# Expert routing of the second layer inside the attention jobs, and expert weights loaded into spent buffers

## The chip, the cores and the metric

The kernel runs on one core of a Trainium2 chip. The metric is the device time of one execution in microseconds (us). Six queues matter: PE (matrix engine; PEld is its weight load), DVE (VectorE), ACT (ScalarE), POOL (GpSimd), and SP, which only issues DMA transfers. ACT and POOL can issue transfers too.

## The reference

Sixteen sequences of 256 tokens with 256 features pass through two layers. Each layer is an attention with a second input, then a gated block of self-attention and experts. Of concern here is the last quarter, the causal self-attention with its mixture of experts:

```
scores = where(causal, q k^T / sqrt(16), min);  o = softmax(scores) v @ w_o     # 16 heads
h      = layernorm(x + o, g1, b1)                       # 4096 rows in all
probs  = softmax(h @ wg);  topv, topi = top_k(probs, 2);  topv /= topv.sum()
y_e    = gelu(h @ w1[e] + bb1[e]) @ w2[e] + bb2[e]      # 8 experts, 256 -> 1024 -> 256, float32
moe    = sum over the 2 chosen experts of topv * y_e
out    = x + tanh(g) * layernorm(h + moe, g2, b2)
```

## The kernel before, in words

**Attention phase** (`attention_phase`). The first three and a half quarters run as 64 jobs: unit u (0 to 3, one for each attention) times sequence b (0 to 15), unit after unit. A job is cut into named steps. `orders()` plans all jobs at once: a greedy list scheduler with a table of costs (`STAGES`) gives every engine a fixed order of steps. Each engine then runs its list strictly in that order and waits on semaphores. Unit 3 is the causal self-attention. Its steps for one sequence: XT, K, Q, V (projections on PE, copied out by ACT), KSPLIT and QSPLIT (POOL cuts a float32 operand into three bfloat16 parts: subtract, cast, subtract), STACKK/STACKQ/ROWSK/ROWSQ (SP writes the parts to memory and reads them back stacked), 16 steps S (scores on PE, masked maximum on DVE), M and MT (maxima folded into the operand), 16 steps T (scores again on PE, exp on ACT, future entries cleared by POOL, line 1248), PV and OT (values, division on DVE), OTT and PROJ (output projection), HNS, HNP, HNX (first layernorm: statistics and scaling on DVE, root on POOL), HNG (multiply by g1, add b1: two POOL instructions, lines 1225 and 1227), HT and HG (gate logits, copied by DVE, line 1475), STOREX (h to memory, line 925). PE may hold scores in two banks only (`S_BANKS`), so it waits for DVE's maximum of two steps ago.

**Routing phase** (`route`, lines 1562 to 1745). After all jobs every engine passes a barrier. The eight experts' weights (16 loads of 512 KB on ACT's queue, 8 of 1 MB on SP's) and two biases `bup` and `bdn` start loading. Meanwhile DVE computes, for 4096 rows at once, the softmax, the best two experts, ranks and running counts; PE names the slots through 64 matmuls of one-hot rows; the result is three tables of 73 columns: `expert_of`, `row_of`, `dest_of`. Slots are packed in tiles of 128 rows, each tile having one expert; there are always 71 tiles.

**Expert phase** (`run_experts`). First SP issues eight loads for the last phase (c_h, c_x, 512 KB each). For each tile POOL copies a column of `row_of`, issues an indirect gather of 128 rows of h, and later copies a column of `dest_of` and scatters the 128 results; between scatter and next gather it waits for the scatter to land (line 1810, 1811). PE turns the rows (line 1835), does 32 matmuls up (line 1846) and 16 down (line 1856); DVE stages the up weights (line 1904), adds biases (1909, 1917); ACT applies gelu. The bodies of two tiles form a hardware loop. `combine` then adds both experts' rows, applies the last layernorm and stores.

## Time and profile before

| | us |
|---|---|
| median of 3 runs | 2578.48 (2577.73 to 2580.44) |
| the profiled execution, its own time | 2577.39 |
| its span in the trace | 2575.0 |
| attention phase ends (gate logits of the last job) | about 1885 |
| routing, up to the first matmul of the first expert tile | 1885 to 1965 |
| expert tiles | 1965 to 2486 |
| combine | 2492 to 2575 |

The profile is one execution. Times in its rows are counted from the start of the span. "Busy" is time in which an engine executes; waiting, register work and DMA issue are not in it. PEclk is the granted TensorE clock, 1.00 being 2.4 GHz and 0.50 being 1.2 GHz. A row of the timeline merges equal instructions that follow each other; the bracket behind it gives the idle time of the engine before it and what ended that.

### The profile page before, as it was taken

The page shows a single profiled execution, that of the slowest core. Times are in us where ns is not written, and L with a number is a line of the kernel's source. Part 1 is how long each engine was busy: PE and PEld are TensorE (multiplying, and loading weights), DVE is VectorE, ACT ScalarE, POOL GpSimd, SP SyncE. Part 2 cuts the span into 40 slices and gives each one's busy share as a digit, 9 for nine tenths or more (in the row PEclk, how much of TensorE's full clock was granted, in tenths as well). Part 3 has the DMA queues.
Part 4 walks back from the last instruction along what each step waited for, and adds up shares of the span by engine and source line. Part 5 has one row for each costly group of instructions (what it writes and reads, how often), then busy time and mean ns, then how long its engine had stood idle before and what let it go on. Part 6 is the DMA issues. An engine that isn't in the chain of part 4 may idle for free. (4 is left out here: it accounts for less than half of the span.)

```text
span 2575.0 us, 52660 instructions
## 1 busy us (share of the span) xinstructions
PE 2187.5 (85%) x17577; PEld 1565.6 (61%) x17578; DVE 1586.2 (62%) x4073; ACT 1388.9 (54%) x2454; POOL 1168.6 (45%) x2040
## 2 busy tenths in 40 slices
PE   1888886988889999989899999999837999999950
PEld 1454454655556655555566666766527999999950
DVE  3788777743444787776777777787554444443337
ACT  3688874544546777776677788777601222222212
POOL 5555423566655553332332347887601333333323
PEclk9999997999999999999999999999956999999985
DMA  6877826325456765555455445556273111111125
GB/s 185 217 190 183 186 76 151 91 89 153 115 155 161 184 179 122 132 129 130 109 134 126 114 110 118 138 123 139 53 231 134 33 36 36 36 35 34 35 84 196
DMA packets 225776, 314.22 MB, mean 122 GB/s; under 512 B 36011, under 2 KB 159911, under 8 KB 219306
## 3 DMA queue, kind: packets, MB, share of 16 engines
q1 hardware_dynamic: 205322, 263.37, 40.7%
q0 software_dynamic: 13728, 35.68, 4.6%
q10 hardware_dynamic: 6528, 12.58, 1.3%
q8 instruction: 118, 1.93, 0.3%
q14 instruction: 80, 0.66, 0.1%
HBM read 215.02 MB, written 98.33 MB: 122 GB/s over the span
## 5 line engine op out<-in xcount | busy, mean ns | idle before, releaser
L1178 ACT ACTIVATE ex<-t_ps 128x512 f32<-128x512 f32 (+1 forms) x1280 | 685.6, 579 | 206.4 <-PE t_ps L1084 152.8
L1494 DVE TENSOR_REDUCE mx<-s_ps 128x2 f32<-128x512 f32 (+1 forms) x1024 | 658.7, 684 | 196.3 <-PE s_ps L1055 114.6
L1084 PE MATMUL t_ps<-qs,ks 123*128 123x256 bf16 x2048 | 363.7, 281 | 28.9 <-ACT ex L1178 14.9
L1107 PE MATMUL pv_ps<-ex,va 128*17 128x256 f32 (+1 forms) x5120 | 324.4, 381 | 1.1 <-POOL ex L1248 0.5
L1846 PEld LDWEIGHTS x_up_ps<-x_rows_t,x_wnow 128*128 128x128 f32 x2272 | 267.3, 193 | 5.3 <-issue 0.9
L1084 PEld LDWEIGHTS t_ps<-qs,ks 123*128 123x128 bf16 x2048 | 174.1, 100 | 157.8 <-ACT ex L1178 75.6
L1846 PE MATMUL x_up_ps<-x_rows_t,x_wnow 128*128 128x128 f32 x2272 | 267.9, 277 | 1.1 <-DVE x_pre L1909 0.7
L1172 ACT ACTIVATE qs<-tr_ps 27x2048 bf16<-27x2048 bf16 x128 | 239.5, 1871 | 52.7 <-PE tr_ps L1068 49.7
L1876 ACT ACTIVATE x_rows_t<-x_rt_ps 128x256 f32<-128x256 f32 x72 | 27.7, 385 | 442.1 <-PE x_rt_ps L1835 442.1
L1856 PE MATMUL x_y_ps<-wdn,x_act 128*128 x1136 | 257.1, 379 | 0.7 <-DVE x_y L1917 0.7
L1061 PE MATMUL s_ps<-ks,qs 99*128 99x256 bf16 (+1 forms) x1024 | 191.9, 290 | 59.9 <-DVE mx L1494 48.5
L1856 PEld LDWEIGHTS x_y_ps<-wdn,x_act 128*128 128x128 f32 x1136 | 210.3, 190 | 26.8 <-issue 1.1
L1055 PE MATMUL s_ps<-ks,qs 96*128 96x256 bf16 x1024 | 184.0, 276 | 34.1 <-DVE mx L1494 30.3
L1107 PEld LDWEIGHTS pv_ps<-ex,va 128*17 128x17 f32 x5120 | 126.3, 99 | 135.5 <-issue 50.1
L1487 DVE CUSTOM_DVE_ANT_0 s_ps<-s_ps,late 128x128 f32<-128x128 f32 (+1 forms) x512 | 167.1, 390 | 44.4 <-PE s_ps L1058 43.8
L1904 DVE COPY x_wnow<-wup 128x1024 f32 x144 | 99.5, 692 | 150.7 <-issue 88.8
L1182 ACT ACTIVATE ot<-pv_ps 128x256 f32<-128x256 f32 x256 | 99.7, 390 | 150.1 <-PE pv_ps L1107 143.7
L1061 PEld LDWEIGHTS s_ps<-ks,qs 99*128 99x128 bf16 (+1 forms) x1024 | 86.5, 101 | 132.3 <-DVE mx L1494 96.3
L1239 POOL TENSOR_TENSOR ak<-ak,pk 128x512 f32<-128x512 f32 x64 | 74.2, 1159 | 164.3 <-ACT pk L1159 102.4
L1256 POOL TENSOR_SCALAR mp<-mx 128x16 bf16<-128x16 f32 x128 | 36.4, 285 | 238.0 <-DVE mx L1494 214.8
L1055 PEld LDWEIGHTS s_ps<-ks,qs 96*128 96x128 bf16 x1024 | 85.8, 98 | 92.8 <-DVE mx L1494 72.6
L1917 DVE TENSOR_TENSOR x_y<-x_y_ps,bdn 128x256 f32<-128x256 f32 x71 | 30.2, 425 | 163.9 <-PE x_y_ps L1856 163.9
(317 smaller groups left out, 3994.0 us busy)
## 6 DMA issues: line engine op xcount, KB each, us to landing
q_parts<-pq SPq DMA_DIRECT2D x128, 192.0 KB
qs<-q_parts SPq DMA_DIRECT2D x64, 384.0 KB
qs<-q_parts SPq DMA_DIRECT2D x192, 128.0 KB
k_parts<-pk SPq DMA_DIRECT2D x96, 192.0 KB
ks<-k_parts SPq DMA_DIRECT2D x96, 192.0 KB
ks<-k_parts SPq DMA_DIRECT2D x288, 64.0 KB
ks<-ctx_k_parts SPq DMA_DIRECT2D x64, 192.0 KB
ks<-ctx_k_parts SPq DMA_DIRECT2D x192, 64.0 KB
```

The costliest lines, as they stand in the source:

```text
L1055: last = pe.matmul(dst[:, r * T:(r + 1) * T], q(src), key(r)[0:rows, h, :], start=True, stop=True)
L1061: last = pe.matmul(dst[:, t * T:(t + 1) * T], q(t), key(0)[0:rows, h, :], start=True, stop=True)
L1084: last = pe.matmul(dst[:, t * T:(t + 1) * T], key[0:ROWS, h, t * P:(t + 1) * P], qs[q_at][0:ROWS, h, :], start=True, stop=True)
L1107: last = pe.matmul(pv_ps[i * VS:i * VS + VW, q0:T], val[:, t, k * QH + i, :], e, start=r == 0 and t == 0, stop=r == srcs - 1 and t == NT - ...
L1172: act.activation(qs[q_at][PRODUCTS:ROWS, k * HG:(k + 1) * HG, :], tr_b[PRODUCTS:ROWS, 0:T].unsqueeze(1).broadcast_to([ROWS - PRODUCTS, HG, ...
L1178: act.activation(ex[:, n % EXPS, 0:w], t_ps[n % 2][:, 0:w], ACT.Exp).then_inc(t_read, 1)
L1182: act.activation(ot[v % 2][:, :], pv_ps[:, 0:T], ACT.Copy).then_inc(pv_read, 1)
L1487: last = dve.tensor_tensor_reduce(out=seen, in0=seen, in1=late[:, 2 * P - w:2 * P], scale=1.0, scalar=FUTURE, op0=ALU.add, op1=ALU.max, ac ...
L1494: dve.tensor_reduce(dst, s_ps[n % S_BANKS][:, :].rearrange("p (a b) -> p a b", a=dst.shape[-1]), AX.X, ALU.max).then_inc(s_read, 1)
L1846: last = pe.matmul(up_ps[h][:, g * P:(g + 1) * P], wnow[k][h][:, c, g * P:(g + 1) * P], rows_t[:, c, :], start=c == 0, stop=c == DC - 1)
L1856: last = pe.matmul(y_ps[:, 0:D], act_t[k][h][:, g, :], wdn[:, bass.ds(x, 1), f, :].rearrange("p e n -> p (e n)"), start=f == 0, stop=f == ...
L1904: dve.tensor_copy(wnow[k][h][:, :, :], wup[:, :, bass.ds(x, 1), h * HALF:(h + 1) * HALF].rearrange("p c e f -> p c (e f)")).then_inc(w_rea ...
```

## The change

1. **Routing goes into unit 3.** `route` is gone. New steps PA, PX, PB, PC, PR, PQ run for groups of sequences, behind sequences 4, 9, 13 and 15 (`PICKS`: 5, 5, 4 and 2 of them). They do the same arithmetic on 128 x (8 experts x 2 tiles x group) elements, with a running count per expert kept from group to group. Each expert has room for all 4096 rows (`ROOM`), so a slot's place is known before later sequences are counted.
2. **Names scattered.** For each tile of 128 tokens and each of two choices a step PS on POOL scatters 128 four-byte row names into a table in memory (`slot_names`, 128 x 256, filled with a "nowhere" value during setup). There are 64 such scatters, 8 of them for the last group.
3. **After the last group** a step PT on DVE makes `expert_of` and `room_of` (the column of the name table that a tile uses). After the barrier POOL waits for all scatters, loads the table, DVE makes `row_of` from it, and a second barrier follows.
4. **Expert phase.** A column's number is now looked up: POOL loads `room_of[n]` into a register before each of its two column copies. The eight c_h and c_x loads are issued once tile 5 or so is done. `bup` and `bdn` are loaded after the attention barrier and waited for by DVE.
5. **Weights early.** Attention buffers (`qs`, `ks`, `ex`, `aq`, `pq`, ..., xt, ctx, w0, w1x) now lie in one `arena`, and the 24 weight loads go into parts of it as those fall dead: steps LWA, LWX, LWK, LWQ, LWP, LWE on SP's queue, from sequence 7 on, the last five after the last PV.
6. **Work moved to VectorE** in unit 3: HNG and QSPLIT go from POOL to DVE.

```diff
+PICKS = {4: 5, 9: 5, 13: 4, 15: 2}
+SCATTER_JOB = 4
...
-    "HNS": [("dve", 1.16)], ... "HNG": [("pool", 2.4)],
+    "HNS": [("dve", 1.16)], ... "HNG": [("dve", 1.25)],
+STAGES_OF_UNIT = {("QSPLIT", 3): [("dve", 1.65)],
...
+    if (u, b) == (3, B - 1):
+        add("LWA", 0, ("PROJ", 2, B - 1, 0), ("VC", 2, B - 1, 0), ("VC", 2, B - 2, 0))
+        add("LWX", 0, *[(n, 3, m, 0) for n in ("Q", "K", "V") for m in range(B - NQ, B)])
+        for m in range(B - NKV, B):
+            add("LWK", m, *[("T", 3, m, (h, 0)) for h in range(H)])
+        for m in range(B - NQ, B):
+            add("LWQ", m, *[("T", 3, m, (h, 0)) for h in range(H)])
+        add("LWP", 0, *[(n, 3, m, 0) for n in ("STACKQ", "STACKK") for m in range(B - NPART, B)])
+        add("LWE", 0, *[("PV", 3, B - 1, n) for n in range(H // QH)])
+    if u == 3 and b in PICKS:
+        s = add("PA", 0, s, *[("HG", u, b - m, 0) for m in range(1, PICKS[b])], past_pick("PC"))
+        s = add("PX", 0, s)
+        for k in range(1 + TOPK):
+            s = add("PB", k, s, past_pick("PQ"))
+        add("PC", 0, s)
+        s = add("PR", 0, s)
+        r = add("PQ", 0, s)
+        for k in range(TOPK * PICKS[b] * NT):
+            needs[("PS", u, scatter_job(b, k), (b, k))] = [r]
...
+                    elif name == "PS":
+                        pool.wait_ge(slots_picked, PICK_NTH[at] + 1)
+                        pool.indirect_dma_start(names_d..., bass.IndirectOffsetOnAxis(ap=p_at[:, m, t:t + 1], axis=0),
+                                                p_names[:, m, t:t + 1], None).then_inc(names_stored, 16)
...
+                    elif name == "QSPLIT":
+                        s.done(dve.tensor_tensor(rest[:, :, :], rest[:, :, :], parts[:, :, 0, :], ALU.subtract))
+                        s.wait()
+                        s.done(dve.tensor_copy(parts[:, :, 1, :], rest[:, :, :]))
+                        s.wait()
+                        dve.tensor_tensor(parts[:, :, 2, :], rest[:, :, :], parts[:, :, 1, :], ALU.subtract).then_inc(late_split, 1)
...
-            route(nc, e)
             run_experts(nc, e)
...
-                sp.wait_ge(a["w_loaded"], 16 * (3 * E + 2))
-                for q in range(RING):
-                    sp.dma_start(flat_pair(a["c_h"][q]), ...
-                    sp.dma_start(flat_pair(a["c_x"][q]), ...
+                sp.dma_start(bup[...], a["b_up"].rearrange("e (f p) -> p (e f)", p=P), allow_slow_non_contiguous=True)...
+                sp.dma_start(bdn[...], a["b_down"].rearrange("e f -> (e f)").partition_broadcast(P))...
+
+            @block.gpsimd
+            def _(pool):
+                pool.wait_ge(a["names_stored"], 16 * TILES * TOPK)
+                pool.dma_start(names[:, 0:ROOMS], a["names_d"]).then_inc(names_loaded, 16)
...
                 def column(z, n):
-                    return z[:, n:n + 1] if isinstance(n, int) else z[:, bass.ds(n, 1)]
+                    at = slice(n, n + 1) if isinstance(n, int) else bass.ds(n, 1)
+                    return z[:, bass.ds(pool.value_load(room_of[0:1, at], min_val=0, max_val=ROOMS), 1)]
```

On POOL, at the end of the attention phase, before (mp, mr: maxima; ex: exponentials; hrstd, o: layernorm of h):

```order
L1248 AFFINE_SELECT ex<-ex 128x2x128 [waits t_read] x6
L1218 TENSOR_SCALAR hrstd<-hmv 128x2 [waits h_moments]
L1220 TENSOR_TENSOR hrstd<-hrstd,power 128x2 [waits pool_step]
L1225 TENSOR_TENSOR o<-o,wexp 128x512 [waits h_normed,norm_loaded]
L1227 TENSOR_TENSOR o<-o,wexp 128x512 [waits pool_step]
L804 UNCONDITIONAL_BRANCH
```

The same place after, down to the table's load behind the barrier:

```order
L1390 AFFINE_SELECT arena<-arena 128x2x128 [waits t_read]
L1345 DMA slot_names<-work 32768x1 [waits slots_picked] x4
L1367 TENSOR_SCALAR hrstd<-hmv 128x2 [waits h_moments]
L1369 TENSOR_TENSOR hrstd<-hrstd,power 128x2 [waits pool_step]
L1345 DMA slot_names<-work 32768x1 [waits slots_picked] x8
L900 UNCONDITIONAL_BRANCH
L1835 UNCONDITIONAL_BRANCH [waits barrier_Pool_Activation_PE_DVE_SP_gather]
L1838 DMA names<-slot_names 128x256 [waits names_stored]
```

The two layernorm instructions have left POOL, and twelve scatters stand at its end, eight of them behind DVE's last PQ.

On DVE, in the middle of a late job of unit 3, before (L1487: masked maximum of a score block; L1466: HNX; L1507 and L1509: division of a head group):

```order
L1507 RECIPROCAL rden<-tr_ps 128x8 [waits stored3,tr_ready]
L1509 TENSOR_TENSOR o<-tr_ps,rden 128x2x64 [waits dve_step]
L1466 TENSOR_SCALAR o<-o,hmv,hrstd 128x256 [waits h_rooted]
L1466 TENSOR_SCALAR o<-o,hmv,hrstd 128x256
L1487 ISA s_ps,mx<-s_ps,late 128x128 [waits s_ready]
```

After, a piece of such a job (L1687: HNX; L1695 and L1697: HNG; L1724: masked maximum; L1712: gate logits; L1532, L1533: first two instructions of a pick):

```order
L1687 TENSOR_SCALAR o<-o,hmv,hrstd 128x256 [waits h_rooted]
L1687 TENSOR_SCALAR o<-o,hmv,hrstd 128x256
L1695 TENSOR_TENSOR o<-o,wexp 128x512 [waits h_normed,norm_loaded]
L1697 TENSOR_TENSOR o<-o,wexp 128x512 [waits dve_step]
...
L1712 COPY work<-pre_ps 128x16 [waits pre_ready0]
L1532 TENSOR_REDUCE work<-work 128x8 [waits pre_read0,pre_read1,dve_step]
L1533 TENSOR_TENSOR work<-work 128x64 [waits dve_step]
L1724 ISA s_ps,mx<-s_ps,late 128x128 [waits s_ready]
```

HNG now stands between HNX and the next maxima, and the pick's instructions stand among the maxima too.

On POOL, in the body of the expert loop, before:

```order
L1797 ISA [waits x_turned]
L1797 COPY x_row_now<-row_of 128x1
L1559 ISA
L1799 DMA x_rows<-h_normed,x_row_now 128x256 [waits x_pool_step]
L1559 REGISTER_ALU
```

After:

```order
L1853 ISA [waits x_turned]
L1853 TENSOR_LOAD room_of
L1853 ISA x2
L1858 ISA
L1858 COPY x_row_now<-row_of 128x1
L1792 ISA
L1860 DMA x_rows<-h_normed,x_row_now 128x256 [waits x_pool_step]
L1792 REGISTER_ALU
```

The lookup stands behind the wait and ahead of the column copy; the scatter's copy has one too.

## Rows read from the trace of the kernel before

**Rows 1.** First section of the page: busy time, share of the span, instructions
```profile
PE 2187.5 (85%) x17577; PEld 1565.6 (61%) x17578; DVE 1586.2 (62%) x4073; ACT 1388.9 (54%) x2454; POOL 1168.6 (45%) x2040
```

**Rows 2.** Stretches: bounds, length, busy PE PEld DVE ACT POOL, PEclk, DMA share, GB/s
```profile
1550.00:1850.00 300.00, 277.49 (x2643) 198.24 (x2643) 224.86 (x1164) 217.65 (x408) 239.37 (x509) 0.99 0.52 119
...
1550.00:1600.00 50.00, 47.75 (x479) 33.46 (x479) 40.32 (x218) 39.77 (x76) 39.05 (x94) 1.00 0.62 134
...
1650.00:1700.00 50.00, 46.99 (x451) 34.01 (x450) 38.28 (x196) 36.30 (x69) 43.40 (x86) 1.00 0.59 127
...
...
1885.00:1965.00 80.00, 30.73 (x135) 29.02 (x135) 46.10 (x111) 0.80 (x2) 4.61 (x11) 0.50 0.85 279
```

**Rows 3.** Timeline from the last job to the first expert tile: start, duration, instruction
```profile
1868.37 0.85 PE L1107 MATMUL pv_ps<-ex,va 128*17 128x256 f32 x16
...
1878.07 1.26 POOL L1225 TENSOR_TENSOR o<-o,wexp 128x512 f32<-128x512 f32 x1 [0.92 <-DVE o L1466]
...
1884.57 0.17 DVE L1475 COPY gate_logits<-pre_ps 128x16 f32<-128x16 f32 x1 [6.64 <-PE pre_ps L957]
...
1896.41 0.42 ACT L1622 ACTIVATE gate_logits<-r_z 128x256 f32<-128x256 f32 x1 [13.87 <-issue]
...
1963.74 0.69 PE L1835 MATMUL x_rt_ps<-ident,x_rows 128*128 128x128 f32 x2 [14.28 <-DMA x_rows<-h_normed,x_row_now]
...
1964.90 6.45 PE L1846 MATMUL x_up_ps<-x_rows_t,x_wnow 128*128 128x128 f32 x32 [0.47 <-ACT x_rows_t L1876]
```

**Rows 4.** Store of h: its 16 issues, with the first and the last start
```profile
L925 SPq DMA_DIRECT2D h_normed<-o x16: 319/338/420, 1573.8 to 1880.7; - x16
```

**Rows 5.** DVE prices: small steps of the routing in a row, then forms by size
```profile
1909.68 0.17 DVE L1693 CAST r_n8i<-r_n 128x8 int32<-128x8 f32 x1
1909.88 0.17 DVE L1694 TENSOR_SCALAR r_n8i<-r_n8i 128x8 int32<-128x8 int32 x1
...
L1670 DVE TENSOR_TENSOR r_z<-r_z,r_first 128x256 f32<-128x256 f32 x2 | 0.8, 424 | 0.1
...
L2014 DVE TENSOR_TENSOR c_h<-c_h,c_x 128x1024 f32<-128x1024 f32 x8 | 9.8, 1225 | 0.3
```

**Rows 6.** One DVE form beside a busy POOL (L1414), beside an idle one (L1991)
```profile
L1414 DVE SCALAR_TENSOR_TENSOR xs<-work,first_share,xs 128x256 f32<-128x256 f32 x64 | 48.7, 800 | 5.0 <-DMA xs<-x 4.4
L1991 DVE SCALAR_TENSOR_TENSOR c_h<-c_y,share_of,c_h 128x256 f32<-128x256 f32 x64 | 26.8, 481 | 3.1 <-DMA c_y<-expert_rows 2.5 <-issue 0.3
```

**Rows 7.** POOL timeline: scatters in a row, and the step into the last phase
```profile
522.50 1.03 POOL L1214 DMA_INDIRECT first_expert_rows<-work,first_dest_of  x1 [0.30 <-issue]
523.83 1.00 POOL L1214 DMA_INDIRECT first_expert_rows<-work,first_dest_of  x1 [0.30 <-issue]
...
2492.32 0.10 POOL L1970 MEMSET c_power<- 128x4 f32 x1 [4.48 <-POOLq L1788]
```

**Rows 8.** Transfers of the biases: size, issue to landing; and the second's issue
```profile
bdn<-in_L_ffn_bb SPq DMA_DIRECT2D x1, 1024.0 KB, 7.0
...
bup<-in_L_ffn_bb SPq DMA_DIRECT2D x1, 32.0 KB, 5.9
...
1887.30 25.85 SPq L1628 DMA_DIRECT2D bdn<-in_L_ffn_bb  x1
```

**Rows 9.** Expert loop: DVE and POOL timeline, then register work of two lines
```profile
2211.71 0.42 DVE L1917 TENSOR_TENSOR x_y<-x_y_ps,bdn 128x256 f32<-128x256 f32 x1 [1.95 <-PE x_y_ps L1856]
2213.90 0.69 DVE L1904 COPY x_wnow<-wup 128x1024 f32 x1 [1.77 <-PE x_up_ps L1846]
...
2210.28 1.00 POOL L1799 DMA_INDIRECT x_rows<-h_normed,x_row_now  x1 [0.79 <-POOL x_row_now L1797]
2212.38 0.18 POOL L1805 COPY x_dest_now<-dest_of 128x1 uint32 x1 [1.10 <-DVE x_y L1917]
...
L1898 DVEq TENSOR_LOAD <-expert_of x214: 297/304/552, 1956.4 to 2480.8; - x107
...
L1810 POOLq FUSED_REGOPS  x1: 37/37/37, 2213.2 to 2213.2; - x1
```

443 lines of the change are left out of this document (245 added, 198 removed).

## The prediction

> **What bounds the kernel now.** I read the sums by engine first, then the stretches, then the timeline where one phase ends and the next begins. No engine is busy all the time: PE has 85% of the span, DVE 62%, POOL 45% [rows 1]. So the stretches decide [rows 2]. From 1550 to 1850, where unit 3 runs, PE is busy for 277.5 of 300 us and POOL for 239.4, DVE for 224.9 (75%): PE sets the pace, and two engines stand close behind. From 1885 to 1965 PE is busy for 30.7 of 80 us at PEclk 0.50 and the DMA engines for 85%. This is routing: the last gate logits end at 1884.57 + 0.17 = 1884.74, the first matmul up starts at 1964.90, a gap of **80.2 us** [rows 3]. Two chains fill it side by side, DVE's arithmetic (ACT's only exp starts 11.7 us late, behind "issue", its 16 weight loads) and the weights themselves. The expert loop is paced by PE again; what matters there is how much slack POOL has.
>
> **The gap at the end of unit 3, part by part.** I count from the same point, the last gate logits.
>
> HNG of the last job lies on this chain. On POOL it is two instructions of 1.26 [rows 3]. On DVE a two-input form of 128 x 1024 takes 1.225 [rows 5], so 128 x 512 is about 0.65 to 0.7, twice 1.4: the point itself comes **1.2 us earlier**.
>
> PA 2, PB 15, PR 6 and PQ 7 instructions of DVE (30 ahead of the last scatters) follow each other at the pace of two small steps, 1909.68 to 1909.88 = 0.20 [rows 5]: 6.2 us. A trip to ACT (0.5) and one to PE (1.4, the wait of the old routing's counts was of that size) make 8.1. Eight scatters on POOL follow at the cadence of the first layer's, 522.50 to 523.83 = 1.33 [rows 7]: 10.6, together 18.7. Then POOL leaves the block. The only row like it, into the last phase, has 4.48 us of idle time under POOL's own queue behind a scatter [rows 7]. It can be as short as a barrier, 0.3; I take 4.4: 23.1.
>
> Behind the barrier SP loads bup and bdn. bup came down in 5.9 us, but bdn's issue stuck for 25.85 behind it [rows 8], in company of 16 weight loads. Alone I take 8 for bup's small pieces and 4 for the 1 MB of bdn (at most its 7.0): 35.1. DVE's lookup (0.6) and x_wnow's copy (0.69) [rows 9] would let the first matmul start at **36.4**. The other chain, the names, runs beside it: 23.1; the table's load 3; conversion 0.5; a second leave behind a load of POOL's own, half of the 4.48, 2.2; a lookup 0.6; barrier to first turn as before, 1956.4 [rows 9] to 1963.74 [rows 3], 7.3; turn and copy 1.2: **37.9**. The names are last, the biases 1.5 behind them. The gap shrinks by 80.2 - 37.9 = 42.3, with HNG's 1.2 by **43.5** (bounds: both leave times 0.3 give 49; biases that take the 25.85 seen give 30). PT, some 6 us of DVE, lies beside the scatters and costs nothing; without them it would add its 6.
>
> The weights are hidden. The arena's last part falls dead with the last PV, 1869.2, 15 us before the gate logits [rows 3], and some 4.5 MB are then still to come: at the 279 GB/s of [rows 2] 16 us, and the gap gives 37 more. If their parts were late, up to 10 us would come back.
>
> **Unit 3: DVE fills up.** Stores of h start from 1573.8 to 1880.7, 16 of them: one job in 20.5 us [rows 4], 14.7 jobs in the 300 us. New on DVE for each job: QSPLIT, 0.69 + 0.42 + 0.69 with gaps 1.9, and HNG 1.4, together 3.3; times 14.7 = 48.5. The picks: 41 instructions for a group of five, some 17 of them of 128 x 80 elements (0.25, between 0.17 for 128 x 8 and 0.424 for 128 x 256 [rows 5]), the others 0.17, with 0.04 between them 9.9 us; the first also sets up its tables (2), the third is smaller (8): 30 in the stretch. DVE's need becomes 224.9 + 48.5 + 30 = 303 us in a stretch of 300: **DVE is the bound**. The highest share that an engine shows in a slice of this unit is PE's 47.75 of 50, 0.955 [rows 2]. At 0.95 the stretch takes 319: +19.
>
> To this comes contention. The same form, 128 x 256 with inputs in SBUF, takes 800 ns where POOL is busy and 481 beside an idle POOL [rows 6], though the first waits on other things too. 0.32 for each of the 5 new large instructions of a job: 14.7 x 5 x 0.32 = 23.5, need 327, at 0.95 the stretch takes 344: +44. I take a third of it, since POOL is relieved of 5 large instructions a job (it gets four scatters of 1.3 for them): 311 / 0.95 = 327, **+27**. Below nothing it can't be unless POOL was the hidden pacer: it was busy for 43.4 of 50 us at most [rows 2], less than PE in every slice.
>
> The Trainium skill speaks against this part: SBUF — State Buffer, "Who interferes with whom", says that a VectorE instruction with two SBUF inputs and a GpSimd instruction that reads SBUF shut each other out, the second waiting for the whole of the first. The trace agrees in kind: 800 against 481 ns for such a form. By the rule in full the stretch has its +44 or more; by a DVE that is left alone, +19.
>
> **Expert loop.** POOL gets two lookups a tile. One on DVE shows as TENSOR_LOAD of 0.304 [rows 9]; with its register work it is 0.6 (three fit in the 1.77 us of idle time before the copy at 2213.90). The gather ends at 2210.28 + 1.00 = 2211.28, DVE's x_y at 2212.13: POOL has 0.85 us of slack before it, and 1.10 idle ahead of x_dest_now [rows 9]. Two lookups would need 1.2, but the second can run while the gather executes: the queue's register work of line 1810 at 2213.2 [rows 9] ran before the scatter had. One lookup, 0.6, is under 0.85: **0** taken. If both count, (1.2 - 0.85) x 70 tiles = +24, with longer lookups +39.
>
> c_h and c_x, 4 MB, now load during the tiles beside gathers; 15 us at 279 GB/s. Between 0 and 10; **+5**, as gathers that queue behind 512 KB transfers hit two tiles. Weight loads stand in SP's queue in unit 3 ahead of rows of q and k: 0 to 8, **+2**. The table's clearing in setup lies on SP beside a longer DVE setup: 0. In `combine` nothing changes.
>
> The Trainium skill, DMA: Bandwidth & Descriptors, "Rules for kernel authors", says that a non-contiguous last dimension becomes one descriptor per element. bup is loaded so, 8192 elements, and bdn's 25.85 us behind it agree with a slow load. By that rule bup stays slow however idle the queues are, which lengthens the gap, not the loop.
>
> **Sum.** The profiled execution took 2577.4 for a span of 2575.0, the median is 1.1 above it. 2577.4 - 43.5 + 27 + 5 + 2 = 2567.9, and 1.1 more: **2569**.
>
> **Rivals.**
>
> *The cover of DVE holds.* DVE's new work falls where it idled, jobs overlap, and the steps are dearer in my count than on the chip (QSPLIT and HNG at 0.6 each, picks at 25). The stretch grows by 0 to 8. For it: DVE has 75 us free in 300. Against it: the need is 303 even uncontended. 2577.4 - 43.5 + 4 + 7 + 1.1 = **2546**.
>
> *DVE saturates below PE's share, with the whole contention.* The masked maxima that hand PE its score banks are DVE's too, two steps ahead only, so each QSPLIT or pick before a maximum stalls PE, which stalls DVE later. Need 327; at 0.955 the stretch takes 342, at POOL's best share, 43.4 / 50 = 0.87, 376: +42 to +76. Taken 0.92: 355, +55. 2577.4 - 43.5 + 55 + 7 + 1.1 = **2597, slower than before**. It decides from a stretch of +42, that is contended instructions at a share of 0.955 or less. For it: the 800 ns, and a strict order on each engine. Against it: POOL is lighter than before.
>
> *POOL bounds the expert loop.* Both lookups come in line with gather and scatter, because the register load waits in the queue: +13 to +39, on the forecast 2582 to 2608. For it: 0.85 us of slack is little. Against it: the register work seen ahead of a scatter.
>
> *The gap doesn't close* (biases stuck behind something, scatters that wait for their descriptors, the leave time doubled): 15 us lost, 2584. It goes into the spread of the forecast.
>
> **How the numbers follow.** The forecast, a gap of 39 to 49 us less, a stretch of +19 to +36 and 0 to 15 elsewhere, gives about 2551 to 2590: chance 0.50. DVE's cover holds: 0.15. DVE saturates: 0.23. POOL bounds the loop: 0.12. A measurement of this kernel can tell about 0.2%, 5.2 us, from no change, so faster is below 2573.3, slower above 2583.6. Faster: 0.38 of the forecast's 0.50 and all of the 0.15, 0.53. Same: 0.09 and 0.02 of the loop's case, 0.11. Slower: 0.03, 0.23 and 0.10, 0.36. The range reaches from 2538, which holds nearly all of the first rival, to 2602, beyond which lie a part of the saturated case and the tail of the loop's, under 0.15. The forecast's own range is 2551 to 2590.
>
> **What would show it.** Gap: last gate logits to first matmul up, 38 instead of 80 us, with eight scatters 1.3 apart and a leave time near 4.4; whichever of names and biases comes last is in the chain. Unit 3: stores of h at a spacing of 22 to 22.5 instead of 20.5, DVE near 95% and PE near 87%; the two-input forms of HNG at 0.7 or at 1.0 tell the contention. Under 21 means that the cover held, over 23.5 that DVE saturates. Loop: the same spacing of tiles, 7.2 us, and idle time left before x_dest_now; none there, with PE waiting for rows, means POOL. c_h: a few us of PE waiting at the tiles behind the sixth. Wrong at its root would be a gap above 50 us, or a unit 3 as long as before with DVE at 95%.

## The result, and the profile after

The changed kernel took **2598.77 us** (median of 6 runs, 2593.92 to 2607.43), the one before 2579.86 beside it (2577.73 to 2586.32). The ratio is 1.0071, 95% interval 1.0051 to 1.0091: 0.7% slower. On another chip, where the kernel before takes 2550 us, the same two gave 1.0016 (1.0003 to 1.0029). The forecast was 2569 and faster; the time lies inside the range of 2538 to 2602, near its top.

The profiled execution has a span of 2595.0 us, 20.0 longer. Cut at three events, the 20.0 come out so:

| us | before | after | difference | forecast |
|---|---|---|---|---|
| start to the last gate logits | 1884.7 | 1935.1 | +50.3 | +27, +2, -1.2 |
| last gate logits to the first matmul up | 80.2 | 40.3 | -39.9 | -42.3 |
| from there to the end | 610.1 | 619.7 | +9.6 | +5 |

The first section of the page answers [rows 1]:

```profile
PE 2190.1 (84%) x17461; PEld 1549.1 (60%) x17462; DVE 1635.0 (63%) x4228; ACT 1385.7 (53%) x2457; POOL 1169.6 (45%) x2022
```

It tells nothing of where 20 us went. The stretches do: first that of [rows 2], then a slice of 50 us in which PE fell back (bounds, length, busy PE PEld DVE ACT POOL, PEclk, DMA share, GB/s):

```profile
1550.00:1850.00 300.00, 267.76 (x2399) 186.14 (x2399) 252.79 (x1184) 200.14 (x375) 207.30 (x440) 0.95 0.55 129
...
1650.00:1700.00 50.00, 43.37 (x353) 29.10 (x353) 43.03 (x206) 27.53 (x53) 33.01 (x69) 0.87 0.44 106
```

PE ran 2399 matmuls in the 300 us that held 2643 before. DVE took more, 252.8 for 224.9, but at 84% it is far from the 95% that the forecast let it reach. And PEclk fell: 0.95 for 0.99, 0.87 in the slice.

The stores of h bound unit 3 better, as they move with it. This row answers [rows 4]:

```profile
L1057 SPq DMA_DIRECT2D h_normed<-o x16: 320/338/420, 1587.2 to 1931.0; - x16
```

343.8 us from the first to the last, against 306.9. The first is 13.4 late already. The last store of x_shifted but one, a step that each job of an earlier unit ends with, starts at 1506.8 before and at 1514.4 after, so 7.7 of that are there already, and the same store three jobs earlier starts at 1403.8 and 1409.6. These 5.8 lie ahead of unit 3's first new step (QSPLIT on VectorE, 1427.1), and they look like spread between traces: on the other chip the two kernels pass that store at 1375.7 and 1376.1, and two more kernels on chips of this kind (e16 and e17 below), with the same work up to there, pass it at 1406.3 and 1397.9.

Between the last gate logits and the expert loop, timeline of DVE, POOL, SP and PE, to be held against [rows 3]:

```profile
1934.90 0.17 DVE L1712 COPY work<-pre_ps 128x16 f32<-128x16 f32 x1 [3.89 <-PE pre_ps L1089]
...
1943.80 1.05 POOL L1345 DMA_INDIRECT slot_names<-work  x1 [15.09 <-DVE work L1568]
...
1953.12 0.96 POOL L1345 DMA_INDIRECT slot_names<-work  x1 [0.31 <-issue]
1963.26 0.39 SPq L1831 DMA_DIRECT2D bup<-in_L_ffn_bb  x1
1963.29 0.61 POOL L1838 DMA_DIRECT2D names<-slot_names  x1 [9.21 <-PEq L1821]
1963.69 5.11 SPq L1833 DMA_DIRECT2D bdn<-in_L_ffn_bb  x1
...
1966.45 0.30 DVE L1845 TENSOR_SCALAR row_of<-names 128x257 int32<-128x257 int32 x1 [16.89 <-DMA names<-slot_names]
1970.23 0.19 POOL L1858 COPY x_row_now<-row_of 128x1 int32 x1 [6.16 <-issue]
...
1974.14 2.74 DVE L1973 COPY x_wnow<-arena 128x1024 f32 x4 [7.40 <-issue]
1974.18 0.69 PE L1903 MATMUL x_rt_ps<-ident,x_rows 128*128 128x128 f32 x2 [33.61 <-DMA x_rows<-h_normed,x_row_now]
```

This part went as forecast: the pick's arithmetic to the first scatter 8.7 us (forecast 8.1), eight scatters 10.3 (10.6), then the two chains side by side: the turning of the first rows, which the names lead to, starts at 1974.18, the first copy of weights, which waits for the biases, at 1974.14. Only the leave time was twice the forecast, 9.21 us of idle POOL for 4.4.

### The profile page after: what moved, and what is told of

It is laid out like the page before. It is cut to its first block and busy times, and to the rows that moved or that the text cites. A ratio compares the mean times of both kernels' runs of the same rounds, so it can differ in the third digit from the quotient of the medians.

```text
span 2595.0 us, 53162 instructions
## 1 busy us (share of the span) xinstructions
PE 2190.1 (84%) x17461; PEld 1549.1 (60%) x17462; DVE 1635.0 (63%) x4228; ACT 1385.7 (53%) x2457; POOL 1169.6 (45%) x2022
## 5 line engine op out<-in xcount | busy, mean ns | idle before, releaser
L1321 ACT ACTIVATE arena<-t_ps 128x512 f32<-128x512 f32 (+1 forms) x1280 | 685.0, 578 | 210.3 <-PE t_ps L1222 156.9
L1222 PE MATMUL t_ps<-arena 123*128 123x256 bf16 x2048 | 366.1, 282 | 30.6 <-ACT arena L1321 18.7
L1245 PE MATMUL pv_ps<-arena,va 128*17 128x256 f32 (+1 forms) x5120 | 329.2, 385 | 3.8 <-POOL arena L1390 3.0
L1315 ACT ACTIVATE arena<-tr_ps 27x2048 bf16<-27x2048 bf16 x128 | 239.5, 1871 | 66.3 <-PE tr_ps L1206 58.1
L1222 PEld LDWEIGHTS t_ps<-arena 123*128 123x128 bf16 x2048 | 174.4, 100 | 161.0 <-ACT arena L1321 79.5
L1924 PE MATMUL x_y_ps<-arena,x_act 128*128 x1136 | 259.0, 381 | 0.7 <-DVE x_y L1986 0.7
L1199 PE MATMUL s_ps<-arena 99*128 99x256 bf16 (+1 forms) x1024 | 193.5, 291 | 62.9 <-DVE mx L1731 49.5
L1924 PEld LDWEIGHTS x_y_ps<-arena,x_act 128*128 128x128 f32 x1136 | 211.4, 191 | 27.3 <-issue 1.1
L1381 POOL TENSOR_TENSOR arena<-arena 128x512 f32<-128x512 f32 x112 | 131.7, 1176 | 196.1 <-ACT arena L1297 112.6
L1193 PE MATMUL s_ps<-arena 96*128 96x256 bf16 x1024 | 184.2, 277 | 33.7 <-DVE mx L1731 30.4
L1724 DVE CUSTOM_DVE_ANT_0 s_ps<-s_ps,late 128x128 f32<-128x128 f32 (+1 forms) x512 | 167.4, 389 | 27.2 <-PE s_ps L1196 25.8
```

The source lines that it names most:

```text
L1193: last = pe.matmul(dst[:, r * T:(r + 1) * T], q(src), key(r)[0:rows, h, :], start=True, stop=True)
L1199: last = pe.matmul(dst[:, t * T:(t + 1) * T], q(t), key(0)[0:rows, h, :], start=True, stop=True)
L1222: last = pe.matmul(dst[:, t * T:(t + 1) * T], key[0:ROWS, h, t * P:(t + 1) * P], qs[q_at][0:ROWS, h, :], start=True, stop=True)
L1245: last = pe.matmul(pv_ps[i * VS:i * VS + VW, q0:T], val[:, t, k * QH + i, :], e, start=r == 0 and t == 0, stop=r == srcs - 1 and t == NT - ...
L1315: act.activation(qs[q_at][PRODUCTS:ROWS, k * HG:(k + 1) * HG, :], tr_b[PRODUCTS:ROWS, 0:T].unsqueeze(1).broadcast_to([ROWS - PRODUCTS, HG, ...
L1321: act.activation(ex[:, n % EXPS, 0:w], t_ps[n % 2][:, 0:w], ACT.Exp).then_inc(t_read, 1)
```

## The experiments

Two kinds of chips turned up, with about 2578 and about 2552 us for the kernel before. In the tables each run is held against a trace of before from its kind: the last gate logits end at 1884.7 on the first, at 1860.8 on the second (e9, the kernel before once more). "Behind" is how much later they end. PEclk is that of the stretch between the first and the last store of h. Each line is one trace. e5 and e12 have the very same unit 3 and e4 differs from it in the weight loads alone; they end at 1895.4, 1896.1 and 1902.4, with 337.4, 338.3 and 341.5 us between the stores, so a difference of a few us between two lines says nothing. Theories A to H are named in the expectations, which use a letter more than once.

### Is it split and scale on VectorE?

**e1** puts both steps back on POOL in the changed kernel, **e2** puts both on VectorE in the kernel before.

```
e1, in the changed kernel:
-"HNG": [("dve", 1.25)]                  +"HNG": [("pool", 2.4)]
-STAGES_OF_UNIT = {("QSPLIT", 3): [("dve", 1.65)], ...
(the bodies of both steps move to POOL with them)
e2, in the kernel before: the same the other way round
```

e1:

> The changed kernel with QSPLIT and HNG of unit 3 back on POOL; all else as changed. In the changed kernel the last gate logits end at 1935.1, 50.3 later than before; this run tells how much of that the two moved steps hold. Theory A (VectorE's added work delays PE, and PE's idle moments bring stretches at half clock): VectorE loses 3.3 us a job, unit 3 ends near 1905 to 1912, half-clock time between 1550 and the end falls from 54.6 us to under 30, total near 2570 to 2575. Rival B (picks, scatters and weight loads hold most): unit 3 ends at 1928 or later, total 2588 or more. Rival C (POOL now fills up: 5.9 us of split and scale plus 5.2 of scatters a job): unit 3 ends later than 1940, total over 2600.

e2:

> The kernel before with QSPLIT and HNG of unit 3 on VectorE; routing, weights and all else as before. Theory A: the two steps alone stretch unit 3 by 15 to 30 us, total 2593 to 2608. Rival B: they alone cost under 8 us, since VectorE has 75 us free in 300 there, total 2578 to 2587, or less as the last job's chain is 1.2 shorter.

Two of the changed kernel's parts were then taken out of unit 3, each for itself. **e3** makes one pick behind the last sequence, **e4** holds all weight loads back.

```
e3: -PICKS = {4: 5, 9: 5, 13: 4, 15: 2}        +PICKS = {15: 16}
e4: -        add("LWA", 0, ("PROJ", 2, B - 1, 0), ...
    +        add("LWA", 0, ("HG", 3, B - 1, 0), ("PROJ", 2, B - 1, 0), ...     (LWX, LWK, LWQ, LWP, LWE alike)
```

e3:

> The changed kernel with one pick of all sixteen sequences behind the last one (so 64 scatters follow it). Its total is longer by design: 56 more scatters of 1.3 are 73 us. What counts is when the last gate logits end. Theory A: unit 3 loses 30 us of VectorE work and all scatters but keeps split and scale: it ends near 1915 to 1925. Rival B: picks and scatters are the main cause, it ends near 1900 or before. If neither matters, 1935.

e4:

> The changed kernel with all 24 weight loads held back until the last gate logits. If the loads on SP's queue or their traffic delay unit 3, it ends earlier than 1935 by what they cost: theory A expects 0 to 3 us, a rival in which SP's order holds back rows of q and k 10 or more. The gap behind it grows: 16.8 MB at 279 GB/s are 60 us against the 40.3 of the changed kernel, so +10 to +25 in total, 2610 to 2625.

| | ratio to before (95%) | gate logits end | behind | stores of h | PEclk |
|---|---|---|---|---|---|
| e9, before | | 1860.8 | | 311.0 | 0.97 |
| e2 | 1.0011 (0.9997 to 1.0026) | 1860.6 | -0.2 | 306.0 | 0.96 |
| e3 | longer by design | 1860.9 | +0.1 | 307.2 | 0.95 |
| e4 | 1.0072 (1.0045 to 1.0099) | 1895.4 | +34.6 | 337.4 | 0.91 |
| e5, changed | 1.0016 (1.0003 to 1.0029) | 1896.1 | +35.3 | 338.3 | 0.92 |
| e1 | 1.0162 (1.0136 to 1.0187) | 1932.7 | +71.9 | 384.2 | 0.86 |

e5 is the changed kernel again, for this kind of chip:

> The changed kernel once more, beside the three kernels of this group, since chips differ: before took 2578 us on one and 2553 on another. Expected ratio to before 1.007, h stores (first to last) 344 us long, 40 us of gap; if this chip is like the second one, 2571 us.

The rows of the stretch between the stores, of e9, e2, e3, e5 and e1, one of each:

```profile
1545.70:1856.70 311.00, 277.94 (x2569) 198.23 (x2567) 215.82 (x1100) 212.22 (x397) 237.38 (x499) 0.97 0.44 105
```

```profile
1550.60:1856.60 306.00, 272.87 (x2511) 192.73 (x2509) 246.51 (x1147) 207.76 (x388) 177.00 (x424) 0.96 0.43 101
```

```profile
1549.70:1856.90 307.20, 273.30 (x2511) 193.36 (x2509) 246.57 (x1146) 207.82 (x387) 176.97 (x424) 0.95 0.59 156
```

```profile
1553.70:1892.00 338.30, 290.17 (x2523) 197.80 (x2521) 273.82 (x1275) 209.62 (x390) 230.84 (x480) 0.92 0.54 142
```

```profile
1544.50:1928.70 384.20, 317.95 (x2580) 210.85 (x2578) 243.01 (x1229) 214.66 (x400) 293.38 (x554) 0.86 0.49 129
```

What follows. Split and scale on VectorE cost **nothing by themselves** (e2: 31 us more busy time on DVE, unit 3 as long; rival B was right there, theory A wrong). Together with the picks and scatters they are even the better place: back on POOL, unit 3 grows by another 37 us (e1), with POOL busy for 293 us and PE waiting for HNG on POOL for 14.0 us. Rival C was right: they make room for the scatters. The weight loads cost unit 3 nothing that a trace can tell (e4 against e5: 0.7 us), and loaded early they are worth 13.6 us of gap (53.6 without, 40.0 with). The total agrees: by the ratios e4 is 0.56%, some 14 us, above e5, inside the +10 to +25 that were expected. With picks and scatters gone from the middle, unit 3 is as short as before (e3), early weights and VectorE's two steps included. So the 35 us hang on picks or scatters in the middle, or on the order that the planner makes with them.

The three rows of e2, e3 and e5 show how the time is lost. e5 has 12 matmuls more than e3 and PE busy for 16.9 us more; PE's idle time grows by 14.2 (from 33.9 to 48.1). In e5 PE worked for 44.7 us at a granted clock of 0.50, in e3 for 20.3. An estimate: at full clock half of the 24.4 between them would be gone, 12.2 of the 16.9. So a bit under half of the loss is waiting, and some 12 to 17 us are the half clock that comes with it.

### Scatters, picks as a block, or wrong costs?

**e6** plans all scatters behind the last gate logits (POOL, which doesn't wait for these, starts the first 6 us ahead of them), **e7** corrects three costs of the planner, **e10** lets other ready steps go ahead of the middle picks', **e11** makes one middle pick.

```
e6:  needs[("PS", ...)] = [r, ("HG", 3, B - 1, 0)], and all of them in job B - 1
e7:  "HNG": 1.25 -> 1.45, ("QSPLIT", 3): 1.65 -> 1.95, "PS": 1.05 -> 1.35
e10: -key=lambda x: (x[1], rank(x[2]), x[0])
     +key=lambda x: (x[1] + (8 for a middle pick's step, else 0), rank(x[2]), x[0])
e11: +PICKS = {9: 10, 15: 6}
```

e6:

> The changed kernel with its picks where they are, but all 64 scatters issued after the last gate logits. Its total is longer by design (56 more scatters in the gap, +73 us). The time from the first to the last store of h tells which of the two holds unit 3 back: 306.9 us before, 343.8 in the changed kernel, 307.2 with picks and scatters both at the end. Theory D (scatters on POOL, 1.0 us busy and 0.3 idle each, stand in front of the clearing of exponentials that PE's value steps need): 305 to 318. Theory A (30 us of picks on VectorE): 335 or more.

e7:

> The changed kernel with three costs in the planner's table set to what the trace shows: a scatter 1.35 instead of 1.05, HNG 1.45 instead of 1.25, QSPLIT 1.95 instead of 1.65. Only orders change. Theory D: if the order is bad because scatters are dearer than planned, h stores take 325 or less instead of 344, total 15 to 20 us under the changed kernel. Rival: POOL's work itself is too much, or each new order is as good or bad as another: 335 to 355, total within 10 us.

e10:

> The changed kernel with one change in the planner: in its choice among ready steps, the steps of the picks behind sequences 4, 9 and 13 count as eight jobs later, so maxima of scores go ahead of them. In the changed kernel a pick stands on VectorE as one block of 12 to 15 us (10.6, 10.2 and 8.0 us of it busy); now 22 to 40 other steps stand between its parts. Theory E (a block longer than PE's two score banks can bridge stops PE for about its length, and PE's idle time brings half clock): first to last store of h 312 to 325 us instead of 338 to 344, total 12 to 25 us under the changed kernel, ratio to before 0.992 to 0.998. Rival A (VectorE's total work counts, wherever it stands): 335 or more, within 5 us of the changed kernel.

e11:

> The changed kernel with one pick in the middle, behind sequence 9 for ten sequences, and the last one for six; longer by design, since 24 scatters and more stand behind the last gate logits (+21 us or more). Theory E: one block of some 17 us in place of three of 12 to 15, so first to last store of h takes 320 to 328 us. Rival A: the work is about 14 us instead of 29, giving 320 too if only the sum counts; the two differ in e10, not here. If orders alone make the 37 us by chance, anything from 307 to 345.

| | ratio (95%) | gate logits end | behind | stores of h | PEclk |
|---|---|---|---|---|---|
| e6 | longer by design | 1900.0 | +39.2 | 344.8 | 0.89 |
| e7 | 1.0089 (1.0054 to 1.0124) | 1912.4 | +51.6 | 372.0 | 0.90 |
| e10 | 1.0095 (1.0071 to 1.0118) | 1914.9 | +54.1 | 364.5 | 0.88 |
| e11 | longer by design | 1883.3 | +22.5 | 328.6 | 0.94 |

Scatters on POOL are not needed for the loss (e6, theory D falls): with 54 of 56 gone from between the stores, POOL is busy for 179 us instead of 231 and unit 3 is no shorter. Truer costs made it worse (e7), and so did spreading the pick (e10, theory E falls): from its first instruction to its last a pick now took 36, 41 and 26 us instead of 14, 12 and 11. One pick in the middle in place of three, half of their time on VectorE and 40 of the 56 scatters, costs two thirds as much (e11).

e7 and e10 say something else too: each changes only the order of steps, and moves the end by 16 and 19 us, which is well beyond the spread of e4, e5 and e12.

### One loss, seen close

The pick behind sequence 4, changed kernel, DVE (L1568 is the pick's last instruction, L1687 HNX, L1695 and L1697 HNG):

```profile
1678.66 1.97 DVE L1557 TENSOR_TENSOR work<-pre_ps,work 128x8 f32<-128x8 f32 x10
...
1682.15 1.05 DVE L1566 CAST work<-work 128x20 f32<-128x20 int32 x1
1683.24 0.18 DVE L1567 TENSOR_SCALAR work<-work 128x20 f32<-128x20 f32 x1
1683.45 0.47 DVE L1568 SCALAR_TENSOR_TENSOR work<-work 128x20 uint32<-128x20 f32 x1
1683.84 1.56 DVE L1687 TENSOR_SCALAR o<-o,hmv,hrstd 128x256 f32<-128x256 f32 x2
1685.51 0.69 DVE L1695 TENSOR_TENSOR o<-o,wexp 128x512 f32<-128x512 f32 x1
1686.23 0.69 DVE L1697 TENSOR_TENSOR o<-o,wexp 128x512 f32<-128x512 f32 x1
```

POOL in the same place (L1381 and L1385: parts of KSPLIT, each a subtraction with two inputs):

```profile
1682.01 1.16 POOL L1381 TENSOR_TENSOR arena<-arena 128x512 f32<-128x512 f32 x1 [0.90 <-ACT arena L1297]
1683.24 0.64 POOL L1383 CAST arena<-arena 128x512 bf16<-128x512 f32 x1
1683.96 1.29 POOL L1385 TENSOR_TENSOR arena<-arena 128x512 bf16<-128x512 f32 x1
```

PE's timeline in the same place, which waits for that HNG:

```profile
1684.14 0.22 PE L1219 MATMUL t_ps<-arena 123*128 123x128 bf16 x1
1687.07 1.02 PE L1077 MATMUL pre_ps<-ident,o 128*128 128x128 f32 x4 [2.71 <-DVE o L1697]
```

And the stretches up to it, during it and behind it:

```profile
1680.30:1683.70 3.40, 3.40 (x33) 2.39 (x32) 3.02 (x10) 2.95 (x7) 2.41 (x4) 1.00 0.00 0
1683.70:1687.10 3.40, 0.69 (x7) 0.36 (x6) 3.23 (x7) 1.85 (x4) 2.84 (x4) 1.00 0.00 0
1687.10:1700.80 13.70, 11.78 (x70) 6.97 (x71) 10.72 (x52) 1.36 (x3) 9.74 (x17) 0.50 0.32 83
```

DVE stood in the pick, so HNX and HNG of another sequence came late, and PE, whose order puts the turning of that h next, stood idle for 2.71 us. More than half of this hole is two DVE instructions that ran long beside POOL's two: the pick's cast at 1682.15, 1.05 us where the next pick's takes 0.18, and the second HNX, 1.24 us of the 1.56 where its like takes 0.41. Together that is 1.7 us. The same cast, as long (1.06 and 1.05 us), stands in e5 and e13.

After the hole the granted clock was 0.50, its lower level of 1.2 GHz, for 13.7 us in which PE was busy for 11.8. The same matmuls (L1089, 128x8) follow each other there at 0.24 us and at 1668 at 0.12, so at full clock this work would have taken about half, an estimate: one hole of 2.7 us cost some 8 here. That is no fixed price. In e5 a hole of the same 2.71 us, in the same place, was followed by 6.8 us at 0.50. In e13 (below), where HNG is nearly empty, the hole is 1.66 us, and 10.2 us at 0.50 follow. In e16, where the pick is empty, PE's longest wait there is 1.4 us, and 10.2 us at 0.50 follow all the same. So emptying one step or the other shortened the hole and did not take the half clock away. The clock was at 0.50 for 17 us of unit 3 before (from 1550 on) and for 60 in the changed kernel.

### Is it VectorE's work, or the order?

VectorE was busy for 0.79 to 0.81 of the stores' stretch in e2, e3, e5 and e11, which looks like a limit. Five kernels were made to test that. **e13** keeps the changed kernel's order and lets HNG touch 8 of 512 elements (part of the layernorm's scaling is left out). **e14** and **e15** stand on **e8**, which keeps routing in one go after the jobs as before, but with the weights in spent buffers, split and scale on VectorE, and the c_h and c_x loads beside the routing; in e14 QSPLIT, in e15 HNG is on POOL again. **e16** keeps the changed kernel's order and all scatters, but the three middle picks do no arithmetic (their tokens get slots by a fixed formula, so their routing is left out).

The changes of e8 and e16 are put in words here:

```
e8:  PICKS = {} ; route() of the kernel before, without its 24 weight loads, c_h and c_x loads behind bdn
e13: -dve.tensor_tensor(rows[:, :, :], rows[:, :, :], g1..., ALU.mult)
     +dve.tensor_tensor(rows[:, 0, 0:8], rows[:, 0, 0:8], g1[:, 0:8], ALU.mult)      (b1 alike)
e16: +if b < B - 1: only the semaphores of PA, PB, PQ; PR copies 8 elements
```

e8:

> Routing after all jobs as before, in one go, but the weights loaded into spent buffers as in the changed kernel, split and scale on VectorE, and the c_h and c_x loads beside the routing. Theory D: unit 3 is as short as before (h stores 305 to 310 us), the exp no longer waits behind 16 issues (-12) and bdn not behind 16 loads, so the gap is 55 to 66 us instead of 80, and the loop is as before: 14 to 25 us faster than before, ratio 0.990 to 0.995. If weight loads hold unit 3 back (rival), h stores take 315 or more and the gain is gone.

e13:

> The changed kernel with the same order of steps, but HNG on VectorE multiplies and adds only 8 of its 512 elements: 16 x 1.3 = 21 us of VectorE work less in unit 3 (part of the layernorm's scaling is left out of what is computed). Theory F (VectorE's busy time over 0.80 sets the length): 274 - 21 = 253, over 0.80 gives 316 us from the first to the last store of h, against 338 to 344. Rival G (the picks' places in the order set it): 330 or more, as the order is the same.

e14:

> Kernel e8 (routing after the jobs, early weights) with QSPLIT of unit 3 back on POOL and HNG left on VectorE. e8 had VectorE busy for 246 us and POOL for 177 in 307; now about 222 and 212. Theory F: VectorE 222 / 0.80 = 278, POOL 212 / 0.77 = 275, below PE's 273 / 0.94 = 291 (270 busy at full clock): 288 to 298 us from first to last store of h, ratio to before 0.988 to 0.992. Rival G: PE and its order set the 307 us in all runs without picks (before 307 to 311, e2 306, e3 307, e8 307), whatever VectorE carries: 304 to 311, ratio 0.995.

e15:

> Kernel e8 with HNG of unit 3 on POOL and QSPLIT left on VectorE: VectorE about 223 us, POOL about 217. Theory F: as e14, 288 to 298 us, ratio 0.988 to 0.992. Rival G: 304 to 311. If the chain at the end matters, this one is 1.2 us worse than e14 in the last job.

e16:

> The changed kernel with its order of steps and all its scatters, but the picks behind sequences 4, 9 and 13 do next to no arithmetic on VectorE (one small instruction in place of some 40; slots of their tokens come from a fixed formula, so the routing of these tokens is left out and the output is not the reference's). About 27 us of VectorE work less, in three places. Theory H (the pick's 12 to 15 us stand in front of HNG or maxima that PE's fixed order wants next; PE stands still for 3 us, and the clock falls to half for some 10 us behind it): last gate logits near 1862 to 1872 instead of 1896, half-clock time in unit 3 under 40 us instead of 60. Rival G (the order itself is bad, whatever stands in the picks): 1885 or later, as with HNG left out (1892).

| | ratio (95%) | gate logits end | behind | stores of h | PEclk |
|---|---|---|---|---|---|
| e8 | 0.9953 (0.9938 to 0.9968) | 1862.6 | +1.9 | 306.9 | 0.96 |
| e13 | work left out | 1891.9 | +31.1 | 334.4 | 0.91 |
| e14 | **0.9895** (0.9862 to 0.9927) | 1849.8 | -11.0 | 305.4 | 0.97 |
| e15 | 1.0011 (0.9993 to 1.0029) | 1880.1 | +19.3 | 323.9 | 0.91 |
| e16 (first kind of chip) | work left out | 1930.5 | +45.8 | 342.5 | 0.90 |

The stretch between the stores in e13, e15 and e16:

```profile
1553.46:1887.89 334.43, 290.51 (x2542) 198.38 (x2530) 259.04 (x1275) 210.24 (x393) 225.43 (x480) 0.91 0.55 144
```

```profile
1552.14:1876.04 323.90, 282.33 (x2492) 196.68 (x2490) 228.38 (x1100) 207.30 (x383) 206.54 (x451) 0.91 0.55 147
```

```profile
1583.90:1926.40 342.50, 293.07 (x2523) 200.06 (x2521) 251.15 (x1175) 209.40 (x390) 232.12 (x480) 0.90 0.54 139
```

The share of 0.80 is not what sets the length (theory F falls). e13 has 15 us less of VectorE work than e5 and unit 3 is 4 us shorter. e16 has 24 us less than the changed kernel (251.2 for 274.8) and is 1.3 us shorter; both are within the spread of like traces, and e16's stores come at nearly the spacing of the changed kernel's. With it theory H falls too: the picks' arithmetic in front of other steps isn't needed for the loss. e15 has neither engine loaded (228 and 207 us in 324) and still loses 19 us. **In these runs taking VectorE's work out of a given order of steps gained next to nothing.** e14 and e15 end 30 us apart. They differ in which of two steps of like size lies on which engine and, with it, in their planned orders; which of the two makes the 30 us was not separated. (Of e14's 12.8 us ahead of e8, 11.3 lie before the first store of h.) What an order alone can do is shown by e7 and e10, 16 and 19 us.

### The other way round: real picks in the good order

**e17** plans as if only the last pick were there, which gives e3's order, and puts the other picks' steps and scatters in by plan time; **e18** does so with e14's placing of QSPLIT.

```
+ORDER = put_picks_in(ORDER, BEGUN, DONE)   # PA at HG + 0.2 us, PB every 2.4 us, PR where both banks are free,
+                                           # scatters every 3.0, 2.0 and 1.4 us
```

(The comment sums up the function.)

e17:

> The changed kernel with all its picks and scatters at work, but the planner plans as if only the last pick and its scatters were there, and a small function then puts the steps of the picks behind sequences 4, 9 and 13 and their 56 scatters into the engines' lists by plan time, spread by 2.4 us. The other steps of each engine stand exactly as in e3, where the last gate logits ended with the kernel before (1861 against 1861). Theory G (the order that a plan with picks makes holds the loss): last gate logits 0 to 15 us behind before on the same kind of chip, ratio to before 0.988 to 0.995. Rival H (picks cost what they hold of VectorE, wherever they stand and whatever the others' order): 25 us or more behind, ratio 1.000 or above, as in e10, where a plan with spread picks gave 54.

e18:

> As e17, with QSPLIT of unit 3 on POOL, so that the order is that of e14's plan, where the last gate logits ended 11 us ahead of before. POOL carries 35 us more beside the scatters, VectorE 23 less. Theory G: last gate logits 10 us ahead to 10 us behind before, ratio 0.984 to 0.993. If POOL's load counts (as the rival for e1, where both steps and the scatters were on POOL, had it), 20 us behind or more, ratio 1.000 or above.

| first kind of chip | ratio (95%) | gate logits end | behind | stores of h | PEclk |
|---|---|---|---|---|---|
| changed kernel | 1.0071 (1.0051 to 1.0091) | 1935.1 | +50.3 | 343.8 | 0.92 |
| e17 | 1.0066 (1.0048 to 1.0085) | 1933.4 | +48.7 | 353.8 | 0.89 |
| e18 | 1.0055 (1.0037 to 1.0073) | 1930.2 | +45.5 | 355.9 | 0.90 |

Theory G, that the planned order alone holds the loss, falls as well: in an order that is worth 0.1 us without picks, real picks and scatters cost as much as in the planner's own. PE waits in e17 for other things than in the changed kernel (waits, longest sums first, stretch 1575 to 1930):

```profile
PE s_ps L1239 <- DVE mx L1768: 17.1, 30, 2.7
PE pv_ps L1289 <- POOL arena L1434: 12.9, 11, 4.1
PE pre_ps L1121 <- DVE o L1741: 6.1, 2, 5.4
```

12.9 us now fall to POOL's clearing of exponentials, for 3.0 in the changed kernel. They fit scatters that the plan had left no room for; that these are what held POOL up is not shown.

### The c_h and c_x loads

**e12** issues the eight loads behind bdn, ahead of the loop.

> The changed kernel with the eight c_h and c_x loads issued right behind bdn, ahead of the expert loop, instead of once the sixth result is done. First to last matmul up took 520.4 us in the changed kernel and 511.7 before; in the trace 6 us of it come in tiles 4 to 12, where the loads are. Expected if they are the cause: 513 to 516 us, total 3 to 6 us under the changed kernel, if the gap doesn't grow (4 MB at 279 GB/s are 15 us, which may delay bdn or the names by some of it). Rival: the loss only moves into the gap, same total.

First to last matmul up took 515.3 us, against 522.1 in e5 (519.1 to 522.1 in all kernels with these loads in the loop) and 511.1 in e9: the loads are worth some 6 us of the loop. But the gap grew to 48.2 from 40.0, and the ratio stayed at 1.0016 (1.0004 to 1.0028). The rows show why (SP and POOL of e12):

```profile
1930.98 5.08 SPq L1833 DMA_DIRECT2D bdn<-in_L_ffn_bb  x1
...
1933.73 0.30 DVE L1848 TENSOR_SCALAR row_of<-names 128x257 int32<-128x257 int32 x1 [16.89 <-DMA names<-slot_names]
...
1939.84 1.14 SPq L1836 DMA_DIRECT2D c_x<-x_shifted  x1
1942.41 0.18 POOL L1861 COPY x_row_now<-row_of 128x1 int32 x1 [11.05 <-issue]
```

The names are ready at 1934.0, but the second barrier waits for SP, which issues until 1941.0.

## Why the prediction was right or wrong

**The gap**: right. Forecast 37.9, measured 40.3, and 39.7 to 40.3 in every kernel that ends with eight scatters, weights early and c loads late. The leave time was 9.2 for the 4.4 taken, and it is no matter of how many scatters stand before it: it was 9.21 behind 24 (e11) and behind 64 (e3, e6) too. Names and biases nearly tied, as said. For the biases 8 and 4 us were taken; bdn landed 9.4 after its issue, 9.8 after bup's. Its issue stood for 5.1 us behind bup, without the 16 loads, for the 25.85 of [rows 8] beside them. HNG on VectorE shortened the last chain as said: 1.41 us in all for two instructions of 1.26 each.

**Unit 3**: wrong, and this turned the sign. The step that failed is "need 303 us in a stretch of 300, so divide by 0.95". It has two faults. First, it took the sum of an engine's work over its best share for the length of a pipeline in strict order: e2 put 31 us on DVE for nothing, e13 and e16 took 15 and 24 us off for 4 and 1. Second, it had no term for the clock. [rows 2] showed PEclk 0.99 in this stretch, and that was there to lose: 14.9 us more of busy PE stand beside 22.0 us more of waiting. What the runs show in the step's place is that moved steps and early weights cost nothing (e2, e3), and that the loss comes with picks and scatters in the middle (e3 against e5), as waiting of PE and as half clock. Nor had the forecast a term for the time ahead of the first store.

**What the 50.3 consist of**, in place of +27: 36.9 in the stores' stretch, of them 22.0 idle and 14.9 PE busy time. PE worked there at 0.50 for 42.6 us after and 9.9 before; half of the difference, 16, is an estimate of what the clock took and covers the 14.9. The other 13.4 lie ahead of the first store, and 5.8 of these look like the spread between traces named above. On the other chip the same two kernels are 35.3 apart, 27.3 between the stores and 8.0 ahead of them. That the forecast's +27 meets this 27.3 is luck: what it was made of, VectorE at 95%, isn't what happened.

**Contention of VectorE and POOL**: small in the sum, not small where it struck. The changed kernel's new two-input forms:

```profile
L1697 DVE TENSOR_TENSOR o<-o,wexp 128x512 f32<-128x512 f32 x16 | 11.7, 734 | 0.5
L1695 DVE TENSOR_TENSOR o<-o,wexp 128x512 f32<-128x512 f32 x16 | 11.4, 712 | 1.7
L1702 DVE TENSOR_TENSOR arena<-arena 128x512 f32<-128x512 f32 x12 | 9.3, 773 | 0.0
```

Undisturbed they take 690 ns. The mean is 0.02 to 0.08 us longer, not 0.32, and over all of them that is some 2 us where the forecast took 8. The 800 against 481 of [rows 6] was contention all the same, and the trace of before shows with which instructions. Two groups of four of that form, and POOL beside the second:

```profile
881.48 1.80 DVE L1414 SCALAR_TENSOR_TENSOR xs<-work,first_share,xs 128x256 f32<-128x256 f32 x4 [1.33 <-DMA xs<-x]
...
907.20 3.82 DVE L1414 SCALAR_TENSOR_TENSOR xs<-work,first_share,xs 128x256 f32<-128x256 f32 x4 [0.82 <-DMA xs<-x]
907.45 1.26 POOL L1239 TENSOR_TENSOR aq<-aq,pq 128x512 f32<-128x512 f32 x1 [0.33 <-ACT pq L1159]
908.77 0.69 POOL L1241 CAST pq<-aq 128x512 bf16<-128x512 f32 x1
909.53 1.21 POOL L1243 TENSOR_TENSOR pq<-aq,pq 128x512 bf16<-128x512 f32 x1
```

Of the 64 such instructions, those beside no POOL instruction took 0.47 to 0.49 us, and 19 took 1.26 to 1.43; each of the 19 began while a two-input TENSOR_TENSOR of POOL on 128x512 was running. In unit 3 after the change POOL has few of these left, and HNG's own are gone from it. It mostly clears exponentials (L1390), and beside that alone the new forms took at most 0.81 us. One of them met a two-input one:

```profile
1546.32 1.16 POOL L1385 TENSOR_TENSOR arena<-arena 128x512 bf16<-128x512 f32 x1
1546.43 1.59 DVE L1702 TENSOR_TENSOR arena<-arena 128x512 f32<-128x512 f32 x1
```

The rule of the Trainium skill (SBUF — State Buffer, "Who interferes with whom"), by which the second of such a pair waits for the whole of the first, is borne out there: of the 1.59 us 0.90 are wait, for the 1.04 that POOL's instruction still ran. Beside the clearing, which reads SBUF too, the trace shows no such wait but at most 0.12 us more, and here the measurement decides. The cast and the HNX in the hole above, one-input instructions, each started while a two-input one of POOL ran and ended within 0.15 us of its end. The same section of the Trainium skill names casts and `tensor_scalar`, which HNX is, among what can contend so, and the trace agrees; no run isolates them. So the price per instruction of the forecast was a mean over a partner that the change itself took away.

**The rivals.** "VectorE saturates" gave 2597 and the time was 2598.8, but by another mechanism: VectorE was at 0.80, not 0.92, and its load is not what counts. That the number fits is luck. Its remark that a pick ahead of a maximum stalls PE comes nearer, but PE's waits for maxima are 11.4 us in e5 and 9.6 in e2, which lost nothing. "The cover holds" was right for split and scale alone (e2) and wrong for the picks. "POOL bounds the loop" was wrong: from the turning of the 12th to that of the 52nd tile's rows the changed kernel keeps its distance to the one before to 0.1 us, so the lookups cost nothing in the steady loop.

**The loop**: +9.6 for +5. 6.0 of it come between the 7th and the 10th tile, where the c loads are, as said and a little dearer; 2.7 come in the last sixteen tiles, where PE waits once more for gathered rows (2.1 us at the 59th), and 0.9 behind them. **Weight loads in SP's queue**: 0.7 us, which is within the spread, forecast 2.

**What stays open.** Picks and scatters out of the middle together: nothing lost (e3). Scatters out alone: no gain (e6). Picks' arithmetic out alone, in the changed order: no gain (e16). Both in, good order: all lost (e17). Picks alone or scatters alone in the good order were not tried, so how the loss divides between them can't be said. Why neither part alone gives anything back, and why the half clock stays when the hole before it goes, is open.

**A version that beats both** came out of the pieces that cost nothing: e14, the old routing, weights loaded into spent buffers, scale on VectorE and split on POOL, 1.05% faster than before (0.73 to 1.38%). Its gap is 64.0 us, 24 more than the changed kernel's, but its unit 3 ends 46 us ahead of it.

## What to carry to other kernels

Work that is taken from a serial stretch and hidden in a tightly scheduled pipeline isn't free because an engine there has idle time. Look for the places where the pacing engine's fixed order wants something behind it, and if that engine runs near its full clock, count the clock as something to lose. Take the price of a contended instruction together with its partner, and ask whether the change keeps that partner. Take a change of many parts apart by where its time lies, not by its sum: here the gain of 40 us was real, and the same gain's cheapest part (early weights) could be had without what ate it. And when an order comes from a planner, compare several plans of the same work before any of them is given a reason: here two changes of order alone moved the end by 16 and 19 us.
